# Second normalisation of a graph network with two expert mixtures: when its first rows are read back and scaled, and when the down weights are zeroed

## The reference

```
xn = layernorm(x)
x  = x + gnn(xn) + mix(xn)             # first half
x  = x + ffn(layernorm(x))             # second half

gnn: 4 experts, each of two layers  relu(mean_over_edges(h) @ Wl + bl + h @ Wr);
     a gate chooses 2 of the 4 experts for each row, out = sum(gate * expert(row))
mix: linear attention, 8 heads, with qkv and output projections
ffn: a shared expert for every row, and 16 routed experts of which each row takes 3;
     an expert is (silu(xf @ gate.T) * (xf @ up.T)) @ down.T
```

## Time and profile before

| what | value |
|---|---|
| median of 3 runs | 1343.03 us (1342.5, 1343.03, 1347.29) |
| the profiled execution | 1341.17 us |
| its span | 1339.5 us |
| TensorE busy | 1246.0 us, 93% |
| VectorE busy | 704.9 us, 53% |
| ScalarE busy | 439.5 us, 33% |
| GpSimd busy | 233.8 us, 17% |
| mean granted clock of TensorE | 0.981 |

### The profile page before, as it was taken

One profiled execution on the slowest core, in us unless ns is written; L12 is line 12 of the kernel. 1 busy time (PEld: TensorE's weight loads), 2 busy tenths in 40 slices (PEclk: granted clock), 3 DMA queues, 4 the chain that ended last, 5 costly groups with the idle time before them and its releaser, 6 DMA issues.

```text
span 1339.5 us, 20390 instructions
## 1 busy us (share of the span) xinstructions
PE 1246.0 (93%) x6004; PEld 969.4 (72%) x6005; DVE 704.9 (53%) x1918; ACT 439.5 (33%) x785; POOL 233.8 (17%) x286
## 2 busy tenths in 40 slices
PE   5999988999999999999999985889999999999994
PEld 3654455787878878887888874668788888887883
DVE  6788855565553463246224425583554455447552
ACT  3333214243352242225222323312342233225331
POOL 2000010015013003300330022116501111110111
PEclk9999999999999999999999998999999999999997
DMA  9600000354344344333434344027763355337522
GB/s 352 234 1 1 1 32 1 107 175 119 118 143 106 121 135 99 87 119 130 106 99 126 113 120 122 1 26 245 208 169 63 56 142 142 56 58 228 139 48 32
DMA packets 72211, 146.62 MB, mean 109 GB/s; under 512 B 11826, under 2 KB 12560, under 8 KB 72148
## 3 DMA queue, kind: packets, MB, share of 16 engines
q1 hardware_dynamic: 54468, 99.41, 21.9%
q0 software_dynamic: 17680, 46.43, 16.4%
HBM read 87.15 MB, written 58.67 MB: 109 GB/s over the span
## 4 chain that ended last, share of the span: by engine, by line
PE 57%; DMA 7%; DVE 5%; issue 3%; POOL 2%; ACT 1%; DVEq 0%; SPq 0%; POOLq 0%; ACTq 0%
PE B L1962 19%; PE B L1814 15%; PE B L1821 8%; PE B L1745 6%; PE B L1898 3%; DMA arow<-counts,idxA 2%; PE B L1845 2%; DMA xg<-slots 2%; POOL slots L720 1%; PE B L1943 1%; DMA out_rows<-y,y_tok 1%; PE B L2004 1%; PE B L1838 1%; PE B L1885 1%; PE B L1583 1%
## 5 line engine op out<-in xcount | busy, mean ns | idle before, releaser
L1962 PE MATMUL B<-GUWH,xtH 128*128 (+1 forms) x344 | 145.5, 423 | 0.8 <-DVE xtL L1416 0.8
L1962 PE MATMUL B<-GUWL,xtH 128*128 (+1 forms) x344 | 136.8, 398 | 0.0
L1962 PE MATMUL B<-GUWH,xtL 128*128 (+1 forms) x344 | 136.6, 397 | 0.0
L711 POOL DMA_INDIRECT out_rows<-y,y_tok x44 | 69.1, 1570 | 377.5 <-ACT y L957 367.4
L1108 DVE TENSOR_SCALAR key<-iota_key,keyT,neg_win 128x320 bf16<-128x320 int16 x240 | 85.2, 355 | 0.0
L1745 PE MATMUL B<-GH,conv 128*128 128x512 f32 x210 | 82.2, 392 | 3.0 <-ACT conv L840 3.0
L1745 PE MATMUL B<-GL,conv 128*128 128x512 f32 x210 | 81.9, 390 | 0.0
L834 ACT ACTIVATE hsXH<-XT 128x512 fp32r<-128x512 f32 x40 | 25.3, 632 | 163.2 <-PE B L1814 161.3
L1962 PE MATMUL B<-DNWH,htH 128*128 x176 | 75.3, 428 | 1.7 <-DVE htL L1416 1.7
L1962 PEld LDWEIGHTS B<-GUWH,xtL 128*128 128x128 f32 x344 | 65.2, 190 | 15.9
L1962 PEld LDWEIGHTS B<-GUWH,xtH 128*128 128x128 f32 x344 | 65.4, 190 | 12.7 <-DVE xtL L1416 0.9
(11 more groups left out here) (371 smaller groups left out, 2792.8 us busy)
## 6 DMA issues: line engine op xcount, KB each, us to landing
raw<-in_L_ffn_expert_gate_up SPq DMA_DIRECT2D x16, 1024.0 KB, 5.3
slots<-fill SPq DMA_DIRECT2D x5, 2112.0 KB, 19.8
hidden<-tr SPq DMA_DIRECT2D x40, 256.0 KB, 2.0
xg<-slots SPq DMA_DIRECT2D x34, 264.0 KB, 2.7
raw<-in_L_ffn_expert_down SPq DMA_DIRECT2D x8, 1024.0 KB, 5.7
counts<-astage SPq DMA_DIRECT2D x10, 648.0 KB, 3.3
W1R<-in_L_gnn_Wr SPq DMA_DIRECT2D x4, 1024.0 KB, 6.1
W1R<-in_L_gnn_Wl SPq DMA_DIRECT2D x4, 1024.0 KB, 8.3
```

The lines of the kernel that those rows point to most:

```text
L711: pool.indirect_dma_start(out=out, out_offset=bass.IndirectOffsetOnAxis(ap=y_tok[:, 0:1], axis=0), in_=y[:, :], in_offset=None, compute_op ...
L1962: last = pe.matmul(bank, rows[a][:, k, :], weights[b](k), start=k == 0 and n == 0, stop=k == KD - 1 and n == 2)
```

## The change

Four things are done:

1. `chosen_slots` works out one more number, in three more VectorE instructions ahead of `gm_slots`: the last expert's first tile plus the smaller of its number of tiles and 3. It stands in a ninth column of `gn_i`. Rows 0 to 383 can stand in no later chosen tile of the last expert than the third.
2. SyncE loads that number and issues the first read (tiles 0 to 2) when that many chosen tiles have been added into `out`; the wait for all of them stands ahead of the second read.
3. VectorE scales the first group (`rows(0)`) ahead of the second group's statistics (`variance(1)`).
4. GpSimd's four memsets of DNW[:, 1] and `ht` stand ahead of its wait for the reads.

```diff
-    gn_i = here("gn_i", [P, 2 * GE], I32)
+    gn_i = here("gn_i", [P, 2 * GE + 1], I32)
...
         wait_first(sp, "ar_in", made * 16 + 32)
-        wait_first(sp, "y2_added", made * 16 + 16)
+        early = sp.value_load(gn_i[0:1, 2 * GE:2 * GE + 1], min_val=GE, max_val=GTILES)
+        wait_first(sp, "y2_added", early * 16 + 16)
         for t0 in range(0, NT - 1, X_TILES):
+            if t0 == X_TILES:
+                wait_first(sp, "y2_added", made * 16 + 16)
             sp.dma_start(X[:, t0:t0 + X_TILES, :],
...
         link(pool.memset(X[96:P, NT - 1, :], 0.0))
         pool.sem_inc(S["x_zero"], 1)
+        for z in [w[:, 1, :, :] for w in DNW] + [h[:, :, :] for h in ht]:
+            pool.memset(z.bitcast(F32), 0.0)
         for t in x_in:
             pool.wait_ge(t, 32)
...
-        for z in [w[:, 1, :, :] for w in DNW] + [h[:, :, :] for h in ht]:
-            pool.memset(z.bitcast(F32), 0.0)
         pool.iota(meta[:, :, 1], pattern=[[0, 2]], base=DUMP, channel_multiplier=1, **imprecise)
...
             variance(0)
-            for c in range(1, len(groups)):
+            rows(0)
+            variance(1)
+            for c in range(2, len(groups)):
                 variance(c)
                 rows(c - 1)
             rows(len(groups) - 1)
...
             dve.tensor_copy(gn_i[:, 0:GE], cnt4[:, 4, :])
             dve.tensor_copy(gn_i[:, GE:2 * GE], cnt4[:, 1, :])
+            link(dve.tensor_scalar(cnt4[:, 2, :], cnt4[:, 1, :], float(X_TILES), None, ALU.min))
+            link(dve.tensor_tensor(cnt4[:, 2, :], cnt4[:, 2, :], cnt4[:, 4, :], ALU.add))
+            dve.tensor_copy(gn_i[:, 2 * GE:2 * GE + 1], cnt4[:, 2, GE - 1:GE])
             link(dve.tensor_scalar(cnt4[:, 5, :], cnt4[:, 4, :], float(P), None, ALU.mult))
```

## The result

The changed kernel takes 0.9974 of the time before, 95% interval 0.9964 to 0.9984: 3.5 us less (2.2 to 4.8). The medians of 20 runs each are 1340.75 and 1344.61 us. Forecast were 4.2 us less, 1338.8 us, range 1335.0 to 1342.8. The time lies within the range, and the move is under the 0.5% named in the forecast. Of the 2.0 us between 1338.8 and 1340.75, 1.6 come from the base: the forecast went from a median of 1343.03 us over 3 runs, and over 20 it is 1344.61. Two of the changed kernel's 20 runs, of 1438.69 us (granted clock 0.842) and 3630.74 us (clock 1.0), are left out of the ratio, and what made them slow stays open (no run of the other kernels is over 1353.3); without them its median is 1340.23.

The account below looks back on a forecast made before the run. TensorE, busy 93% of the span, and its waits around the second normalisation bound the kernel. Stage -4.7 plus 0.5 for three instructions gives -4.2 us: 1338.8 us against the 1343.03 median, range 1335.0 to 1342.8.

Parts of the forecast that it names:

- VectorE's path: Second normalisation up to tile 3's scaling: early read 3.14 plus memsets 3.27, less 0.18 and 0.7, gains 5.5 us.
- B: Rival, chance 0.18: memsets collide again, by a late add or GpSimd's timing; gain 1.9 to 3, time 1340.5 to 1341.6 us.
- C: Rival, chance 0.07: early read does not come early, memsets free; gain 1.5 to 2.8 us, time 1341.2.
- The early read: Second normalisation: read issued about 819, statistics begin at 825.87 behind VectorE's weight blocks, not 829.01; gain 3.14 us.
- The memsets: First group's scalings and L1023 lose 3.27 us to memsets; moving them saves this, new meetings cost 0.7, bounds 0 and 3.0.
- The order: Scaling group 0 before group 1's statistics keeps VectorE's total but uncovers ScalarE's root: +0.18 us; second read hidden.
- TensorE and ScalarE next: Copies wait for group 1's root; TensorE at half clock, back on the way: turning 3 at 839.3, gain 4.7 us.
- Everything behind it moves one for one: Behind the turning of tile 3 (844.02), counts and waits move along, so a gain there runs to the end undiminished.
- The three instructions: Ahead of gm_slots: 0.47 us on the path, nothing covers it; +0.5 us, bounds 0.2 and 2.0.
- the signs that would have made the forecast wrong: Scalings still over 2 us, last add over 7 us, or something behind turning 3 giving the gain back.
- D: Rival, chance 0.03: slower, early read delays the last add over 7.8 us and the second read bounds; 1345.4 at 15 us.
- A: Rival, chance 0.15: clock or ScalarE do not bind, little memset loss; stage gain 6.2 us less 0.5, time 1337.3.

Follow-up runs that it names:

- experiment 7: Also written act: the changed kernel with ScalarE's deviation(1) ahead of tile 2's copy, not tile 0's; ratio 0.9961, stage 37.6 us.
- experiment 8: The changed kernel with the four memsets behind the last scaling; ratio 0.9954, stage 36.8 us.
- experiment 1: The kernel before with only the ninth column of gn_i allocated, nothing written there; ratio 1.0003, stage 40.4 us.
- experiment 2: Also written order: the kernel before with rows(0) ahead of variance(1) and nothing else; ratio 0.9986, stage 41.6 us.
- experiment 5: The changed kernel without the early read: the first read waits for all chosen tiles as before; ratio 0.9991, stage 40.0 us.
- experiment 6: Also written three8: the kernel before with 16 linked VectorE instructions of the added kind ahead of gm_slots; ratio 1.0038, 5.1 us more.
- actlate: The changed kernel with deviation(1) ahead of tile 2's copy and memsets behind the last scaling, three instructions still in chosen_slots; ratio 0.9935, stage 35.6 us.
- early: The kernel before with only the early read and its count, order and memsets as before; ratio 0.9979, stage 38.6 us.
- after: The changed kernel itself, in its profiled execution, against the kernel before; 1340.3 us, ratio 0.9974 over the runs.
- best: The changed kernel with deviation(1) ahead of tile 2's copy, memsets behind the last scaling, three instructions moved into VectorE's gather wait; ratio 0.9969, stage 37.1 us.

## Why the prediction was right, and where it was off

The terms of VectorE's path and the next bound were right in kind. Two costs were set too small: the meetings with the memsets and TensorE's half clock. The time could not tell this: the range holds every gain from 0.2 to 8 us over the median that the forecast started from, and rivals B and C with it. By the terms as the profiles measured them the change would be -2.5 us; that the runs gave -3.5, nearer to the -4.2 of the forecast, is luck as far as the rows can tell.

- **The early read**: right. Issue at 2.0 us behind the product, start of the statistics limited by the weight blocks, gain 3.26 forecast 3.14.
- **The memsets**: the mechanism right, the size wrong. 3.27 us went, but where I took 0.7 for new meetings it was 1.55 (and 1.95 in experiment 7). The number that failed is the last add's landing: I stayed a little over the case in which it does not move, and it moved by 1.7 us. With it the first large memset lies on L1017, the second on L1026. I had bounds that hold this, 0 to 3.0. That the shift makes the difference is read from these rows and not tested by itself; that the memsets do is experiment 8, which gives 1.4 us back on VectorE's path.
- **The order**: +0.18 right (L1017 to L1023 is 0.96 with the 0.47 in it, so 0.49). VectorE's path: 3.26 + 3.27 - 0.18 - 1.55 = 4.8, measured 26.32 - 21.51 = 4.81. By experiment 1, 3.27 is what this one profile lost to the memsets; another of the same code lost 1.6.
- **TensorE and ScalarE next**: right as the new bound, by `deviation(1)` ahead of copy 0; experiments 2, 5, 7 show it. Here too the size was off: I took the clock to come back on the way. It stayed at 0.50 up to turning 3 and past it, so 23.36 and not 22.2 (0.85 of the 1.15 is the memsets' shift, the rest is the clock), and logits 2 ran partly at that level: the distance from turning 3 to the first shared matmul is 15.7 us against 15.07 where the clock is full. "Everything behind it moves one for one" failed by these 0.6 us.
- **The three instructions**: 0.46 us in the trace (3.50 against 3.04), forecast 0.47, on the path (experiment 6).
- **The sum**: -2.95 + 0.46 = -2.5 us by the profiles, -3.5 (2.2 to 4.8) by the runs, -4.2 forecast. The profiles' stage before is one draw: with experiment 1's 40.4 the gain of the stage would be 1.4 us, less 0.46. So the sum of the profiles is less sure than the runs, and the 1 us between -2.5 and -3.5 is accounted for by no row.
- **Rivals**: B describes what happened as well as the forecast does. Its mechanism is there (a late add, a large memset each on L1017 and L1026), and so are its numbers: 1.9 to 3 us for the stage, measured 2.94; 1340.5 to 1341.6 us, measured 1340.75. The forecast had 4.7 us for the stage. Of the signs that would have made the forecast wrong two stayed out, if by little: the scalings took 1.88 us (over 2 was named) and the add 6.78 (over 7). The third, a loss behind turning 3, came in a small way, the 0.6 us of the clock. D's mechanism is there too, but the add is 1.7 us late, far from the 7.8 at which it would decide. A's 6.2 us for the stage need both the pause and the meetings gone: actlate has 42.0 - 35.6 = 6.4. C and the layout fall.

## What to carry to other kernels

An engine's in-order program has to be reordered together with that of its partner: VectorE's new order was worth nothing that these profiles show until ScalarE's waits followed it. Work of GpSimd belongs where VectorE has nothing on the path; moving it out of one place of meeting put it into three smaller meetings, with its own trigger delayed by the same change. For changes of 0.3%, distances within a stage, taken over several profiles, tell more than the whole time or a single profile.

## What the runs showed of the hardware

- A large memset of GpSimd (2048 elements for each partition) alone takes 1.80 us. VectorE steps of 3 elements, 0.17 us elsewhere, took 1.61 us beside one (early), 1.44 (order), 1.04 (act), 0.83 and 0.64 (after). Which step is hit is decided by tenths: the unchanged code lost 3.1 us in one execution and 1.6 in another.
- An indirect add of 0.26 MB, measured from its issue to the memset that waits for it, took 5.07 us alone (4.76 to 5.07 in six profiles) and 6.78 beside a read of 0.77 MB issued 0.27 us ahead of it (5.98 to 7.17 in eight).
- After a wait of 2.12 us TensorE came back at 1.2 GHz in one execution (best; 1.12 us for a turning), and after 1.68 us at 2.4 GHz in another (actlate; 0.66) of the same code in this stage: worth 1.4 us. After 2.62 us it came back at 2.4 GHz (act). At 200 to 250 us the granted clock is 0.93 in seven profiles and 0.97 in seven, and with 0.93 the last product ends 3.5 us later in the mean (three8 less its 3.2 us).
